# Attention in groups of three rounds, three buffers of q and k loaded one head further ahead, the row maxima spread over the whole head

## The reference

```python
h = layernorm(x) * (1 + ca) + sa
q, k, v = split(h @ Wqkv.T + bqkv)            # 16 heads of 32 channels
att = softmax(where(causal, rope(q) @ rope(k).T / sqrt(32), -inf))
x = x + ga * ((att @ v) @ Wo.T + bo)          # ga: gate of the batch
h = layernorm(x) * (1 + cb) + sb
p = softmax(where(kept, h @ gate.T, -inf))    # top 8 of 48 kept experts
x = x + gb * sum over the 8 of  weight * (silu(h Wg) * (h Wu)) Wd
```

## Time and profile before

| | |
|---|---|
| median of three executions | 4264.32 us |
| span of the profiled execution | 4268.8 us |
| a regular pair of heads in batch 0 (heads 5 and 6) | 72.3 us |
| a pair of heads beside a set of inverses (heads 3 and 4) | 74.5 us |
| PE busy over the span | 3857.2 us, 90% |
| DVE, POOL, ACT busy | 2754.6, 2780.5, 1806.6 us |

### The profile page before, as it was taken

How to read it: one execution, slowest core, us unless ns; L and a number is a source line. 1 busy time by engine, 2 the same in 40 slices (tenths; PEclk the granted TensorE clock), 3 DMA queues, 4 the chain that set the end, 5 groups by cost and what they waited for, 6 DMA issues and landing times. The chain is left out here.

```text
span 4268.8 us, 81098 instructions
## 1 busy us (share of the span) xinstructions
PE 3857.2 (90%) x21344; PEld 2337.8 (55%) x21344; DVE 2754.6 (65%) x5889; ACT 1806.6 (42%) x3526; POOL 2780.5 (65%) x2251
## 2 busy tenths in 40 slices
PE   5989999987999999879899999879899999859998
PEld 2754544456744454457554544457545444547776
DVE  3767677466757767476667776567676774645655
ACT  1345555423355555332355555233455555211111
POOL 3768788824668878716678888427687888215554
PEclk8989999998999999989899999889899999979999
DMA  6543333242533333334433333425333332349997
GB/s 210 180 119 91 91 99 108 79 181 98 178 93 100 86 102 96 120 135 148 139 91 100 99 98 108 155 82 179 115 90 91 99 105 81 102 135 258 258 257 190
DMA packets 305135, 549.12 MB, mean 129 GB/s; under 512 B 59572, under 2 KB 99636, under 8 KB 301492
## 3 DMA queue, kind: packets, MB, share of 16 engines
q1 hardware_dynamic: 283192, 485.62, 37.8%
q0 software_dynamic: 21504, 58.40, 5.8%
HBM read 311.86 MB, written 174.85 MB: 114 GB/s over the span
## 5 line engine op out<-in xcount | busy, mean ns | idle before, releaser
L1141 ACT ACTIVATE Pt<-PS 128x512 f32<-128x512 f32 (+3 forms) x2560 | 1205.9, 542 | 1004.6 <-PE PS L1334 554.9
L1006 POOL TENSOR_TENSOR Sm<-Pt 128x512 f32<-128x512 f32 (+3 forms) x960 | 1029.5, 1078 | 389.6 <-ACT Pt L1141 383.6
L1653 DVE TENSOR_REDUCE part<-PS 128x1 f32<-128x512 f32 x1536 | 1003.5, 685 | 334.6 <-PE PS L1311 329.6
L1311 PE MATMUL PS<-QK 96*128 96x512 f32 (+3 forms) x2560 | 1026.8, 419 | 88.6 <-DVE mT L1668 24.4
L1334 PE MATMUL PS<-QK 97*128 97x512 f32 (+3 forms) x2560 | 991.8, 409 | 38.7 <-DMA QK<-mT 18.5
L1358 PE MATMUL PS<-Pt,V 128*32 128x512 f32 (+3 forms) x5120 | 870.0, 554 | 42.5 <-POOL Sm L1006 42.3
L1362 PE MATMUL PS<-Sm,onesv 128*32 128x512 f32 (+3 forms) x1920 | 818.8, 535 | 0.0
L1649 DVE CUSTOM_DVE_ANT_0 PS<-PS,consts 128x128 f32<-128x128 f32 (+3 forms) x1024 | 503.8, 495 | 415.8 <-PE PS L1311 408.5
L1334 PEld LDWEIGHTS PS<-QK 97*128 97x128 f32 x2560 | 488.0, 193 | 474.7 <-issue 345.7
L1006 POOL TENSOR_TENSOR Sm<-Sm,Pt 128x512 f32<-128x512 f32 (+1 forms) x640 | 713.2, 1114 | 50.2
L1311 PEld LDWEIGHTS PS<-QK 96*128 96x128 f32 x2560 | 496.0, 195 | 299.5 <-DVE part L1653 110.8
(11 more groups left out here) (169 smaller groups left out, 4962.6 us busy)
## 6 DMA issues: line engine op xcount, KB each, us to landing
QK<-qkd SPq DMA_DIRECT2D x720, 128.0 KB, 3.1
qkd<-st SPq DMA_DIRECT2D x64, 1024.0 KB, 4.5
Wg<-wgu SPq DMA_DIRECT2D x48, 768.0 KB
o<-od SPq DMA_DIRECT2D x448, 64.0 KB, 2.0
W<-wd SPq DMA_DIRECT2D x3, 6144.0 KB, 21.5
Wd<-wdn SPq DMA_DIRECT2D x48, 384.0 KB
xin<-x SPq DMA_DIRECT2D x16, 1024.0 KB, 7.9
vd<-vst SPq DMA_DIRECT2D x16, 1024.0 KB, 6.1
```

The source lines that it names most:

```text
L1006: nc.gpsimd.tensor_tensor(total, of[0][:, first:CH] if i == 1 else total, of[i][:, first:CH], ALU.add).then_inc(sum_done, 1)
L1141: nc.scalar.activation(Pt[:, t % NPT, first:CH], S2[t % NS2][:, first:CH], ACT.Exp, scale=SCALE).then_inc(exp_done, 1)
L1311: mm(s1[:, 0:w], QK[0:3 * HD, hh % 2, 0, qb * P:(qb + 1) * P], QK[0:3 * HD, hh % 2, 1, c * CH:c * CH + w], start=True, stop=True).then_inc ...
L1653: v.reduce_max(part[:, qb, cc:cc + 1], s1[:, 0:w], AX.X).then_inc(s1_dve, 1)
```

## The change

Five things are done in the stream, and the memory is laid out anew for them:

1. Groups of three rounds (`BURST = 3`): 7, 8, 9, 9 and 7 score tiles in the five groups of a head, with the max tiles between them, then the values of the three rounds before. `NPT` goes from 12 to 18 tiles, `NSM` from 4 to 6, `LAG` from 3 to 5.
2. Three buffers of q and k (`QKB`), filled a head earlier: when the scores of head h-1 are done, SP loads head h+1 instead of head h. At the start of a batch SP loads heads 1 and 2 one after the other, ahead of the row of head 0's second half.
3. The max tiles of the next head are spread over all 15 rounds of a head; those of head 1 begin at round 6 of head 0 instead of round 4.
4. The copies of sums leave the ends of the groups: a chunk's copy stands behind the fourth score tile (`COPY_BEHIND = 3`) of the group two after the one with the chunk's last round. By the groups of three and the new `LAG`, the four reciprocals of a chunk, two and two in neighbouring groups before, fall into one group.
5. In the last head the "out" steps of the output projection have other rounds (`OUT_AT`), and the first half of it and the sets of scale and copy fall into groups of three.

```diff
-NPT, NSM, LAG = 12, 4, 3
+BURST, NBUF = 3, 3
+NPT, NSM, LAG = 18, 6, 5
...
-TILES_FROM = 2
-FIRST_TILES_FROM = 4
-OUT_AT = (10, 10, 11, 12, 13, 14, 15, 16)
+FIRST_TILES_FROM = 6
+COPY_BEHIND = 3
+OUT_AT = (10, 10, 11, 12, 14, 15, 15, 16)
...
-        late = TILES_FROM if hh > 1 else FIRST_TILES_FROM
-        at, span = NR * (hh - 1) + late, NR + 1 - late
+        late = 0 if hh > 1 else FIRST_TILES_FROM
+        at, span = NR * (hh - 1) + late, NR - late
...
-            closing[n].append(("copy", hh, j))
+            copies[(NR * hh + LAST_ROUND[j]) // BURST + 2].append(("copy", hh, j))
...
-    for n in range(0, NR * H + 12, 2):
+    for n in range(0, NR * H + 12, BURST):
+        late = copies[n // BURST]
         if n < NR * H:
-            here = [divmod(n, NR), divmod(n + 1, NR)]
+            here = [divmod(n + i, NR) for i in range(BURST)]
             tiles = [("score", hh, r, k) for hh, r in here for k in ROUNDS[r][1]]
-            aside = beside[n] + beside[n + 1]
+            aside = sum(beside[n:n + BURST], [])
             for i in range(max(len(tiles), len(aside))):
                 out += tiles[i:i + 1] + aside[i:i + 1]
+                if i == COPY_BEHIND:
+                    out += late
             out += [("plus", *of) for of in here]
-        if 2 <= n < NR * H + 2:
-            out += [("value", *divmod(n - 2, NR)), ("value", *divmod(n - 1, NR))]
-        out += closing[n] + closing[n + 1]
+        if BURST <= n < NR * H + BURST:
+            out += [("value", *divmod(n - BURST + i, NR)) for i in range(BURST)]
+        if n >= NR * H:
+            out += late
+        out += sum(closing[n:n + BURST], [])
...
+                def load_stack(hh):
...
                 for hh in range(1, H + 1):
                     g, h = divmod(hh, GH)
                     if hh >= 2:
 
                         wait_apart(sp, s2_ready, NPT_B * b + NTILE * (hh - 1))
-                    if hh < H:
-                        for j in range(NCH):
-                            stack(hh, j, qkd[b, g, h * HD:(h + 1) * HD, :, j * CH:(j + 1) * CH])
+                    if hh == 1:
+                        load_stack(1)
+                    if hh + 1 < H:
+                        load_stack(hh + 1)
                     max_row(hh - 1, 1)
```

More of the change, by code:

```diff
@@ L97, with stacked @@
 NCK = NCH * NG
+def stacked(i):
+    return len(range(i, H, NBUF))
 def extent(j, k):
@@ L163, in stream @@
     beside = [[] for _ in range(NR * H)]
+    copies = [[] for _ in range(NR * H // BURST + 4)]
     negated = {}
@@ L379, in adaln_block @@
         rsA = place("rsA", [P, TPC], F32)
+        XIN_AT = at[0]
         xin = [place("xin0", [P, TPC, C], F32), xin1]
@@ L385, in adaln_block @@
         at[0] = W_AT
-        Pt = place("Pt", [P, NPT, CH], F32)
-        Sm = place("Sm", [P, NSM, CH], F32)
+        Pt0 = place("Pt0", [P, 12, CH], F32)
+        Sm0 = place("Sm0", [P, 4, CH], F32)
         o1 = place("o1", [P, T], F32)
@@ L390, in adaln_block @@
         assert at[0] <= W_END
+        at[0] = C_END
+        Sm1 = place("Sm1", [P, 2, CH], F32)
+        Pt1 = place("Pt1", [P, 1, CH], F32)
+        assert at[0] <= W_AT
+        at[0] = XIN_AT
+        QK2 = place("QK2", [P, 2, T], F32R)
+        Pt2 = place("Pt2", [P, 5, CH], F32)
+        PT_END = at[0]
+        Pt = [of[:, i] for of, n in ((Pt0, 12), (Pt1, 1), (Pt2, 5)) for i in range(n)]
+        Sm = [of[:, i] for of, n in ((Sm0, 4), (Sm1, 2)) for i in range(n)]
+        QKB = [QK[:, 0], QK[:, 1], QK2]
         at[0] = OD_AT
@@ L433, in adaln_block @@
         at[0] = PHASE
-        x1 = place("x1", [P, 2, TPC, C], F32)
         xn = place("xn", [P, TPC, C], F32)
         h2 = place("h2", [P, TPC, C], F32)
+        x1 = place("x1", [P, 2, TPC, C], F32)
         h2T = place("h2T", [P, KT, CH], F32)
@@ L539, in adaln_block @@
         v_in = [sem("v_in0"), sem("v_in1")]
-        qk_in = [[sem("qk_in%d%d" % (i, j)) for j in range(NCH)] for i in range(2)]
+        qk_in = [[sem("qk_in%d%d" % (i, j)) for j in range(NCH)] for i in range(NBUF)]
         s1_ready = sem("s1_ready")
@@ L697, in stack @@
                     for blk, pair in enumerate((parts[:, 0::2], parts[:, 1:3], parts[:, 0::3])):
-                        sp.dma_start(QK[blk * HD:(blk + 1) * HD, hh % 2, :, cols].bitcast(F32), pair).then_inc(qk_in[hh % 2][j], 16)
+                        sp.dma_start(QKB[hh % NBUF][blk * HD:(blk + 1) * HD, :, cols].bitcast(F32), pair).then_inc(qk_in[hh % NBUF][j], 16)
                 def store_parts(n):
@@ L735, in max_row @@
                     wait_apart(sp, mt_ready, 2 * (H * b + hh) + half + 1)
-                    sp.dma_start(QK[3 * HD:3 * HD + 1, hh % 2, 0, half * (T // 2):(half + 1) * (T // 2)].bitcast(F32),
+                    sp.dma_start(QKB[hh % NBUF][3 * HD:3 * HD + 1, 0, half * (T // 2):(half + 1) * (T // 2)].bitcast(F32),
                                  mT[:, half].bitcast(F32)).then_inc(mrow_in[half], 16)
@@ L787, in _ @@
                     wait_apart(sp, v_out[i], 32 * (NCH // 2) * (b + 1))
+                def load_stack(hh):
+                    g, h = divmod(hh, GH)
+                    for j in range(NCH):
+                        stack(hh, j, qkd[b, g, h * HD:(h + 1) * HD, :, j * CH:(j + 1) * CH])
                 for hh in range(1, H + 1):
@@ L964, in _ @@
                         wait_apart(pool, rope_mul, 2 * NCK * (b + 1))
-                        nc.gpsimd.memset(QK[3 * HD:3 * HD + 1, 1, 1, :].bitcast(F32), 1.0).then_inc(ones_set, 1)
-                        wait_apart(pool, ones_set, 3 * b + 3)
+                        wait_apart(pool, v_out[1], 32 * (NCH // 2) * (b + 1))
+                        for i in range(1, NBUF):
+                            nc.gpsimd.memset(QKB[i][3 * HD:3 * HD + 1, 1, :].bitcast(F32), 1.0).then_inc(ones_set, 1)
+                        wait_apart(pool, ones_set, 4 * b + 4)
                     elif kind == "mul":
@@ L999, in _ @@
                             pool.wait_ge(pv_done, ONE + NV * b + at - NSM + 1)
-                        of = [Pt[:, (NTILE * hh + tile_at(j, k)) % NPT] for k in ks]
+                        of = [Pt[(NTILE * hh + tile_at(j, k)) % NPT] for k in ks]
                         for i in range(1, len(ks)):
                             first, _ = extent(j, ks[i])
-                            total = Sm[:, at % NSM, first:CH]
+                            total = Sm[at % NSM][:, first:CH]
                             if i == 2:
@@ L1140, in _ @@
                             act.wait_ge(pv_done, ONE + NV * b + NR * ((t - NPT) // NTILE) + ROUND_OF[(t - NPT) % NTILE] + 1)
-                        nc.scalar.activation(Pt[:, t % NPT, first:CH], S2[t % NS2][:, first:CH], ACT.Exp, scale=SCALE).then_inc(exp_done, 1)
+                        nc.scalar.activation(Pt[t % NPT][:, first:CH], S2[t % NS2][:, first:CH], ACT.Exp, scale=SCALE).then_inc(exp_done, 1)
                     elif kind == "normed":
@@ L1333, in _ @@
                             pe.wait_ge(exp_done, ONE + NPT_B * b + t - NS2 + 1)
-                        last = mm(S2[t % NS2][:, first:CH], QK[0:3 * HD + 1, hh % 2, 1, k * P:(k + 1) * P],
-                                  QK[0:3 * HD + 1, hh % 2, 0, j * CH + first:(j + 1) * CH], start=True, stop=masked == 0)
+                        last = mm(S2[t % NS2][:, first:CH], QKB[hh % NBUF][0:3 * HD + 1, 1, k * P:(k + 1) * P],
+                                  QKB[hh % NBUF][0:3 * HD + 1, 0, j * CH + first:(j + 1) * CH], start=True, stop=masked == 0)
                         if masked:
@@ L1361, in _ @@
                             mm(O[j % 2][3 * HD:P, firsts[0]:firsts[1]], onesv[:, :], of[0][:, firsts[0]:firsts[1]], start=begins, stop=False)
-                        mm(O[j % 2][3 * HD:P, firsts[1]:CH], onesv[:, :], Sm[:, at % NSM, firsts[1]:CH], start=begins, stop=r == LAST_ROUND[j]).then_inc(pv_done, 1)
+                        mm(O[j % 2][3 * HD:P, firsts[1]:CH], onesv[:, :], Sm[at % NSM][:, firsts[1]:CH], start=begins, stop=r == LAST_ROUND[j]).then_inc(pv_done, 1)
                     elif kind == "out":
```

19 lines of the change are left out of this document (11 added, 8 removed).

## The result

The changed kernel takes 4409.91 us (median of four executions, 4408.8 to 4416.3), the kernel before 4263.57 beside it: a ratio of 1.0345, 95% interval 1.0331 to 1.036. It is slower by 146 us where 78 was forecast, and 5 us beyond the upper end of the range. The sign and most mechanisms were as forecast. One cost, the wait for a row of maxima in three heads of each batch, stood in no term of the sum, and the terms of the first head and of the inverses had the wrong size.

What follows compares the result with a forecast made beforehand. PE's order was taken to bound the heads. Per batch -7 + 8.7 + 13.3 + 4.5 = +19.5 us, four times +78, gave 4342 us; range 4240 to 4405.

Steps and rivals of the forecast that it cites:

- the wait for SP's row: Rival: the second half's row, behind loads and moves, comes 1 us late in each head; 56 us more, 4398; chance 0.12.
- First head: Start of each batch's stream: second dozen loads delay the row, and maxima crowd DVE; +13.3 us per batch (+6 to +15).
- The row's 7.8: Head 0: the second twelve loads stand ahead of the row of maxima in SP's queue, adding 7.8 us with nothing hiding it.
- The rest was put at 5.5: Rest of head 0: three groups of 13.3 maxima on DVE take 28.8 us, 5.5 more than 23.25.
- Regular heads: Fourteen heads per batch: changes of kind, earlier loads, copy and maxima give -0.5 us per head (-2.6 to +1.1), -7 per batch.
- The changes of kind: PE in regular heads: 2.5 fewer pairs of changes between bursts and values, 0.40 us each; -1.0 us per head.
- The copy amid the burst: Groups 3 and 4 of a head: PE waits on score banks 0.3 to 0.8 us each; +1.1 us per head.
- Inverses: Beside each set: four reciprocals in one gap overrun DVE, 5.7 us against 2.8; +8.7 us per batch (+4 to +13).
- Last head: End of the stream: chunk 0's scale stands behind six additions, delaying PE's first output projection; +4.5 us per batch (-1 to +8).

Runs made afterwards that it cites:

- the run with the row first: Changed kernel with SP sending the second half's row of maxima ahead of the twelve loads in every head; 4295.66 us, ratio to the kernel before 1.0076.

## Why the prediction was wrong

**Where it failed: the sum has no term for the wait for SP's row.** The prediction had this wait as a rival only, "1 us late in each head", with a chance of 0.12, and against it "as ordered, the row stands directly behind the loads". In a regular head the row is in time even behind the loads: putting it first changed the other heads from 1 on by 0.4 us at most. It is late where the loads are late, and these stand behind everything that SP has in the head before: in heads 5, 9 and 13 a store that waits for POOL's scale. The prediction named SP's queue ahead of the row but didn't follow what stands ahead of the loads in the three heads behind a set; and it saw that six additions come ahead of the scale in the last head, but not that the same order holds for the sets within the stream. Moving the row gave 21.9 us per batch back in these heads, 88 us of 146.

**First head: 18.2 us instead of 13.3.** The row's 7.8 were right (7.3 in the trace; 7.5 per batch when the second dozen was moved). The 12 DMAs' issue costs what the earlier trace rows said, 0.63 to 0.65 us each on SP. The rest was put at 5.5, for DVE with 13 max tiles per group; it is 10.9. Mending it took both an earlier begin of the maxima (3.5 us) and groups of two at the start (6.0), which bring part of the values ahead of the scores that take the row. The prediction said PE's only other work were the max tiles. It missed the values of rounds 0 to 2, which the groups of three had put behind the waiting scores, and it worked with durations at full clock, where the trace has stretches at 0.50 right behind the wait and three times later.

The Trainium skill ("DMA: Bandwidth & Descriptors", section "Issuing engines are not separate DMA queues") calls the sequencer's time for a DMA usually small relative to the DMA itself. For one load the trace agrees: 0.63 us on SP, against a median of 3.2 from issue to landing in the page of the changed kernel's profile. Twelve of them in order ahead of a row that PE waits for cost 30 us in four batches all the same.

**Regular heads: right in sign, half the size.** Without the rows' waits (the run with the row first), the pairs without a set take 71.3 us against 71.9 before, -0.27 per head where -0.5 was put, within its bounds. The changes of kind were worth 0.76 us per head in these pairs for the 1.0 priced (1.09 over all heads), and the rest of the change took some of it back. The copy amid the burst was put at 1.1 and is 0.3 at most. Heads 13 and 14 took 74.6 us before and 71.3 in that run; the prediction has no term for these 3.3, and why the pair was long before was not followed up.

**Inverses: wrong.** Beside a set a pair takes 2.2 us more than one without in the run with the row first, and 3.2 more before, where 5.7 and 2.8 were put: per batch -3 instead of +8.7. DVE does run late behind four reciprocals, but PE waits for it only where a max tile needs a bank, 0.8 us in the rows above, not 1.75. Even the bound "0 if the banks' slack takes it all" lies above what came.

**Last head: right in mechanism and nearly in size**, +3.4 for +4.5. By itself the scale behind six additions costs 7.9. What gave the other 4.5 back was not taken apart: groups of three against two are worth 3.2 of it with the scale mended, and the moved projections were not tried alone.

So errors of both signs met: per batch 22 us not priced, 5 too few at the start, 11 too many in the heads and 1 at the end. They cancel in part, so it is luck that the sum of 78 missed by 68 us and not by more.

## What to carry to other kernels

A DMA queue that one engine issues in order is an engine like any other: for each transfer that something waits for, list what stands ahead of it, and for each of these what *it* waits for. A prefetch that isn't urgent belongs behind a small transfer that is. Longer groups save changes between kinds of work in the steady state and cost at its ends, where work that could have filled a wait is now behind it; the two can have different group sizes. When groups grow, look in every place at what they put ahead of a step that another queue waits for: the same six additions were priced in the last head and overlooked in three others.

## What the runs showed of the hardware

Issuing a load of 128 KB held SP 0.63 to 0.65 us at the stream's start, whether 12 or 24 followed each other (7.79 and 15.19 us), and up to 0.79 in the rows of head 5 (9.45 us for twelve). A matmul of the value pass took 1.07 us in the rows at half clock (granted 0.50, 1.2 GHz) and 0.60 to 0.63 at full (1.00, 2.4 GHz). After 18.6 us of standing PE worked on at 0.50 for 4.6 us and then had 1.00, after 4.5 us of standing for 5.2 us: in these two rows of batch 0 the longer stand made the return no longer. Behind the long one the clock fell to 0.50 three times more before head 1, each time at the end of a burst in which max tiles had waited for DVE, or right behind it; in the kernel before it did not fall there. What decides it was not tried.
